# A decoder layer's self-attention: P.V in two passes over stacked high and low values, the output product behind the projection unit, and the latents turned one batch later

## What is computed

```
q = (x @ Wq.T).reshape(b, t, H, DH).transpose(0, 2, 1, 3)      # 32 heads of 16
k = (x @ Wk.T).reshape(b, t, HKV, DH).transpose(0, 2, 1, 3)    # 8 key/value heads of 16
v = (x @ Wv.T).reshape(b, t, HKV, DH).transpose(0, 2, 1, 3)
q = q * cos + _rotate_half(q) * sin
k = k * cos + _rotate_half(k) * sin
scores = jnp.einsum('bhgtd,bhkd->bhgtk', qg, k) / math.sqrt(DH)
attn = jax.nn.softmax(jnp.where(causal, scores, min), axis=-1)
ctx = jnp.einsum('bhgtk,bhkd->bhgtd', attn, v)
return ctx.transpose(...).reshape(b, t, E) @ Wo.T
```

## Time and profile before

| | |
|---|---|
| median of 3 runs | 1007.19 us (1006.62 to 1007.50) |
| the profiled execution | 1007.50 us, of which its span 1005.8 us |
| PE busy | 995.6 us (99% of the span) |
| DVE, ACT, POOL busy | 641.4, 559.5, 519.8 us (64%, 56%, 52%) |
| self-attention's batches | from 37.7 us to about 287 us, 29.83 us each in the middle |
| granted TensorE clock | 0.999 of full speed |

### The profile page before, as it was taken

One profiled execution on the slowest core, in us unless ns is written; L12 is line 12 of the kernel. 1 busy time (PEld: TensorE's weight loads), 2 busy tenths in 40 slices (PEclk: granted clock), 3 DMA queues, 4 the chain that ended last, 5 costly groups with the idle time before them and its releaser, 6 DMA issues.

```text
span 1005.8 us, 16102 instructions
## 1 busy us (share of the span) xinstructions
PE 995.6 (99%) x5552; PEld 836.7 (83%) x5552; DVE 641.4 (64%) x1224; ACT 559.5 (56%) x1695; POOL 519.8 (52%) x529
## 2 busy tenths in 40 slices
PE   8999999999999999999999999999999999999997
PEld 7777777777788888888888888888888888899996
DVE  6888888888433786555655655555555566655654
ACT  5766667666534665555656556555655667422221
POOL 3645444444231786665755756576666568512220
PEclk9999999999999999999999999999999999999999
DMA  9410111104454313233213313322332245100000
GB/s 343 119 29 15 43 42 44 42 22 124 135 157 119 95 57 102 74 95 105 86 61 105 105 64 106 92 76 94 95 105 75 83 139 168 62 22 21 21 22 21
DMA packets 74857, 85.15 MB, mean 85 GB/s; under 512 B 4512, under 2 KB 54688, under 8 KB 74784
## 3 DMA queue, kind: packets, MB, share of 16 engines
q1 hardware_dynamic: 74784, 84.21, 26.2%
HBM read 65.32 MB, written 18.87 MB: 84 GB/s over the span
## 4 chain that ended last, share of the span: by engine, by line
PE 92%; DVE 3%; ACT 2%; DMA 1%; issue 1%; POOL 1%; SPq 1%; DVEq 0%; POOLq 0%; ACTq 0%
PE bank L237 23%; PE bank L239 22%; PE bank L238 22%; PE bank L1143 11%; PE bank L1187 5%; PE bank L903 3%; PE bank L864 1%; PE bank L868 1%; DMA rawO<-in_L_attn_Wo_dram 1%; PE bank L871 1%; PE bank L874 1%; ACT Pb L1424 0%; DVE Kbdl L1696 0%; PE bank L817 0%; PE bank L810 0%
## 5 line engine op out<-in xcount | busy, mean ns | idle before, releaser
L673 POOL TENSOR_TENSOR Pb<-Pb,b_rec 128x512 f32<-128x512 f32 x128 | 135.5, 1059 | 200.6 <-DVE b_rec L1848 200.5
L1424 ACT ACTIVATE Pb<-bank,b_nb 128x256 f32<-128x256 f32 x256 | 119.1, 477 | 14.3 <-DVE b_nb L1843 14.2
L1843 DVE TENSOR_REDUCE b_nb<-bank 128x2 f32<-128x512 f32 x128 | 88.1, 688 | 59.2 <-PE bank L239 58.4
L635 POOL TENSOR_TENSOR Pa<-Pa,a_rec 128x512 f32<-128x512 f32 x64 | 68.2, 1066 | 102.1 <-DVE a_rec L1727 101.5
L1342 ACT ACTIVATE Pa<-bank,a_nb 128x128 f32<-128x128 f32 x256 | 90.8, 370 | 45.5 <-DVE a_nb L1721 44.8
L1285 ACT ACTIVATE PTh<-bank 128x512 fp32r<-128x512 f32 x128 | 76.3, 596 | 67.1 <-PE bank L1187 67.1
L237 PE MATMUL bank<-WOh,Oh 128*128 128x512 f32 x256 | 111.3, 435 | 0.0
L1597 DVE TENSOR_TENSOR PTl<-bank,PTh 128x512 fp32r<-128x512 f32 x128 | 87.7, 686 | 22.3 <-ACT PTh L1285 22.2
L239 PE MATMUL bank<-WOh,Ol 128*128 128x512 f32 x256 | 101.0, 395 | 0.0
L238 PE MATMUL bank<-WOl,Oh 128*128 128x512 f32 x256 | 100.4, 392 | 0.0
L1285 ACT ACTIVATE Oh<-bank 128x512 fp32r<-128x512 f32 x64 | 38.3, 599 | 91.4 <-PE bank L239 91.4
(11 more groups left out here) (279 smaller groups left out, 3008.6 us busy)
## 6 DMA issues: line engine op xcount, KB each, us to landing
KV<-kv_scratch SPq DMA_DIRECT2D x64, 512.0 KB, 3.4
kv_scratch<-KVst SPq DMA_DIRECT2D x64, 256.0 KB, 3.1
raw<-in_L_xattn_Wo_dram SPq DMA_DIRECT2D x32, 256.0 KB, 3.9
raw<-in_L_xattn_Wq_dram SPq DMA_DIRECT2D x24, 256.0 KB, 3.2
cx<-in_ctx_dram SPq DMA_DIRECT2D x8, 256.0 KB, 8.9
raw_first<-in_L_xattn_Wq_dram SPq DMA_DIRECT2D x8, 256.0 KB, 4.6
raw<-in_L_ffn_up_w_dram SPq DMA_DIRECT2D x8, 256.0 KB, 3.9
raw<-in_L_ffn_down_w_dram SPq DMA_DIRECT2D x8, 256.0 KB, 3.5
```

Source lines behind the costliest of these rows:

```text
L635: gp.tensor_tensor(pj, pj, a_rec[:, SG * j:SG * j + SG].unsqueeze(2).to_broadcast([P, SG, P]), ALU.mult).then_inc(g_norm, 1)
L673: gp.tensor_tensor(pk, pk, b_rec[:, k % 4, :].unsqueeze(2).to_broadcast([P, 2, KEYS]), ALU.mult).then_inc(b_g_norm, 1)
L1424: op = act.activation(Pb[:, k % 4, h, :], bank[k % 3][:, h * KEYS:(h + 1) * KEYS], ACT.Exp, bias=b_nb[:, k % 4, h:h + 1], scale=1.0, accum ...
L1843: dve.tensor_reduce(b_nb[:, k % 4, :], bank[k % 3][:].rearrange("p (h k) -> p h k", h=2), AX.X, ALU.max, negate=True).then_inc(b_v_nb, 1)
```

## The change

- **Values.** `Vst` replaces `Vbdh` and `Vbdl`: one 128 by 128 block for each head, the head's high parts at its own 16 columns and its low parts 64 columns away. For j from 0 to 3 the high parts fill rows 0 to 63 of bank 7 and the low parts rows 64 to 127; for j from 4 to 7 bank 4 takes it, the other way round. So a step has two products, with PTah and with PTal, in place of three.
- **Fold.** ACT copies the rows with the low parts (OLa, OLb), and `add_low(n)`, a product of 64 rows with a swapped identity (L960 of the changed file), adds them to the other half of the bank: `add_low(0)` at step 6, `add_low(1)` behind `scores(b + 1, 0)`. ACT and DVE then split each half of 64 partitions (OTh, OTl have tiles of their own now).
- **Order at the end of a batch.** The tail unit stands ahead of the output product and waits for OTl's first half; the output product waits for the second.
- **Latents.** `turn_latents(b)` moves from the end of batch b to step 2 of batch b + 1 (in the last batch to step 0, where ACT evicts it ahead of probabilities 3); ACT's and DVE's parts move along. `turn_xn` goes ahead of the unit of step 0, and its eviction and low part go forward: DVE's `xnTl` stands ahead of reciprocal 2.
- **Keys.** `turn_k` uses bank 3. The fourth block of Kbdl is made by POOL behind `normalise(b, 2)`.
- **Behind the last batch** `first_queries(1)` and `(2)` each stand one place further forward, and SP's load of `gate_w` waits for the output product instead of P.V.

```diff
-        VBW = P + SD
-        Vbdh = sb("Vbdh", "F", 0, [SKV * VBW], F32R)
-        Vbdl = sb("Vbdl", "F", 4.5, [SKV * VBW], F32R)
-        OTh, OTl = PTah[:, 0, :], PTal[:, 0, :]
+        Vst = sb("Vst", "F", 0, [SKV, P], F32R)
+        OTh = sb("OTh", "F", 4, [D], F32R)
+        OTl = sb("OTl", "F", 6, [D], F32R)
+        swap_r = sb("swap_r", "ST", 6, [P], F32R)
+        LOWER, UPPER = slice(0, 64), slice(64, P)
+        OLa, OLb = OTl[UPPER, :], PTah[LOWER, 0, :]
...
                 for j in range(2, SKV):
                     normalise(b, j)
+                    if j == 2:
+                        gp.wait_ge(v_qkl, 2 * b + 2)
+                        src = f32(KTl[:, KC - 1, :]).unsqueeze(1).to_broadcast([P, SG, P])
+                        gp.tensor_tensor(Kbdl[:, KC - 1, :].rearrange("p (c k) -> p c k", c=SG), src,
+                                         bd_mask[:].unsqueeze(2).to_broadcast([P, SG, P]), ALU.mult).then_inc(g_kbl, 1)
...
             def turn_k(b):
                 pe.wait_ge(v_qr, 2 * b + 2)
+                if b:
+                    pe.wait_ge(a_exp, SKV * b)
                 for m in range(KC):
-                    op = pe.transpose(bank[4][:, m * P:(m + 1) * P], kr[:, m * P:(m + 1) * P], ident[:])
+                    op = pe.transpose(bank[3][:, m * P:(m + 1) * P], kr[:, m * P:(m + 1) * P], ident[:])
...
-                pe.wait_ge(v_kbd, KC * b + m + 1)
+                if m < KC - 1:
+                    pe.wait_ge(v_kbd, (KC - 1) * b + m + 1)
+                else:
+                    pe.wait_ge(g_kbl, b + 1)
...
                 def values(j):
+                    bk = bank[7] if j < 4 else bank[4]
                     if j == SKV - 1:
                         for n, split in enumerate((v_ptl_half, v_ptl)):
                             pe.wait_ge(split, SKV * b + SKV if n else b + 1)
                             cols = slice(n * KEYS, (n + 1) * KEYS)
-                            op = split3(pe, bank[7][:, cols], Vbdh[:, j * P:(j + 1) * P], Vbdl[:, j * P:(j + 1) * P],
-                                        PTah[:, j % 2, cols], PTal[:, j % 2, cols], False, n == 1)
+                            pe.matmul(bk[:, cols], Vst[:, j, :], PTah[:, j % 2, cols], start=False, stop=False)
+                            op = pe.matmul(bk[:, cols], Vst[:, j, :], PTal[:, j % 2, cols], start=False, stop=n == 1)
                         op.then_inc(pe_pv, 1)
                         return
                     pe.wait_ge(v_ptl, SKV * b + j + 1)
@@ -919,8 +945,20 @@
                         pe.wait_ge(v_vl, b + 1)
                         pe.wait_ge(v_ul, U_B0 + 2 * b)
-                    op = split3(pe, bank[7][:], Vbdh[:, j * P:(j + 1) * P], Vbdl[:, j * P:(j + 1) * P],
-                                PTah[:, j % 2, :], PTal[:, j % 2, :], j == 0, False)
+                    if j == 4:
+                        pe.wait_ge(a_exp, SKV * b + 6)
+                    pe.matmul(bk[:], Vst[:, j, :], PTah[:, j % 2, :], start=j % 4 == 0, stop=False)
+                    op = pe.matmul(bk[:], Vst[:, j, :], PTal[:, j % 2, :], start=False, stop=j == 3)
+                    if j == 3:
+                        op.then_inc(pe_pv, 1)
+                def add_low(n):
+                    pe.wait_ge(a_ol, 2 * b + n + 1)
+                    bk, rows, low = ((bank[7], UPPER, OLa), (bank[4], LOWER, OLb))[n]
+                    pe.matmul(bk[:], swap_r[rows, :], low, start=False, stop=True,
+                              skip_group_check=True).then_inc(pe_sw, 1)
...
                         pe.wait_ge(v_qkl, 2 * b + 1)
+                        pe.wait_ge(v_vl, b + 1)
+                        if not last:
+                            if b == 0:
+                                pe.wait_ge(v_ctl, 6)
+                            else:
+                                turn_xn(b + 1)
                         unit(U_B0 + 2 * b)
-                        if not last:
-                            if b:
-                                pe.wait_ge(v_htl, b)
-                            else:
-                                pe.wait_ge(v_ctl, 6)
-                            turn_xn(b + 1)
+                        if b == 0:
+                            turn_xn(1)
+                        if last:
+                            turn_latents(b - 1)
                         scores(b, 2)
...
                         q_product((0, 1))
+                        if b:
+                            turn_latents(b - 1)
                     if j == 3:
                         scores(b, 3)
                         if not last:
                             q_product((2, 3))
                     if j == 4 and not last:
+                        if b:
+                            pe.wait_ge(v_htl, b)
                         kv_product(range(KC))
                     if j == 6 and not last:
                         turn_q(b + 1)
+                    if j == 6:
+                        add_low(0)
...
+                add_low(1)
+                tail = U_E0 - 1 if last else U_B0 + 2 * b + 1
+                pe.wait_ge(v_ol, 2 * b + 1)
+                if b:
+                    pe.wait_ge(v_htl, b)
+                unit(tail)
+                pe.wait_ge(v_ol, 2 * b + 2)
                 for g in range(SG):
-                    if g % 2 == 0:
-                        pe.wait_ge(v_ol if g else v_ol_half, b + 1)
                     op = split3(pe, bank[6][:], OTh[:, g * P:(g + 1) * P], OTl[:, g * P:(g + 1) * P], SOh[:, g, :],
                                 SOl[:, g, :], g == 0, g == SG - 1)
                 op.then_inc(pe_wo, 1)
                 if not last:
                     scores(b + 1, 1)
-                unit(U_E0 - 1 if last else U_B0 + 2 * b + 1)
-                if not last:
-                    pe.wait_ge(v_vl, b + 2)
-                else:
+                if last:
                     first_queries(0)
+                    first_queries(1)
                     pe.wait_ge(v_ul, U_L0 + 7)
-                turn_latents(b)
...
-            first_queries(1)
+            first_queries(2)
             pe.wait_ge(v_htl, NB)
             unit(U_E0)
             unit(U_E0 + 1)
@@ -1100,7 +1154,6 @@
             unit(U_E0 + 2)
             unit(U_E0 + 3)
             unit(U_E0 + 4)
-            first_queries(2)
             first_queries(3)
...
                     hi(PTah[:, j % 2, :], bank[5 + j % 2][:]).then_inc(a_pt, 1)
+                    if j == 0 and last:
+                        latents_hi(b - 1)
+                    if j == 0 and b and not last:
+                        xn_hi(b + 1)
+                    if j == 5:
+                        act.wait_ge(pe_pv, 2 * b + 1)
+                        hi(OLa, bank[7][UPPER, :]).then_inc(a_ol, 1)
+                    if j == 7:
+                        if not last:
+                            k_hi(b + 1)
+                        act.wait_ge(pe_sw, 2 * b + 1)
+                        hi(OTh[LOWER, :], bank[7][LOWER, :]).then_inc(a_o, 1)
                     if j + 3 < SKV:
                         probs(b, j + 3)
                     if j == 0:
                         unit_hi(U_B0 + 2 * b)
-                        if not last:
-                            xn_hi(b + 1)
+                    if j == 0 and b == 0:
+                        xn_hi(1)
+                    if j == 2 and b and not last:
+                        latents_hi(b - 1)
                     if j in LAST_STEPS and last:
                         unit_hi(LAST_STEPS[j])
                     if j == 6 and not last:
                         q_hi(b + 1)
-                if not last:
-                    k_hi(b + 1)
-                act.wait_ge(pe_pv, b + 1)
-                hi(OTh, bank[7][:]).then_inc(a_o, 1)
+                act.wait_ge(pe_pv, 2 * b + 2)
+                hi(OLb, bank[4][LOWER, :]).then_inc(a_ol, 1)
                 if not last:
                     values_hi(b + 1)
+                act.wait_ge(pe_sw, 2 * b + 2)
+                hi(OTh[UPPER, :], bank[4][UPPER, :]).then_inc(a_o, 1)
+                if not last:
                     for j in range(3):
                         probs(b + 1, j)
                 else:
@@ -1376,7 +1444,8 @@
                         first_wq(h)
                     unit_hi(U_L0 + 6)
                 unit_hi(U_E0 - 1 if last else U_B0 + 2 * b + 1)
-                latents_hi(b)
+                if last:
+                    latents_hi(b)
...
+                cells = Vst[:].rearrange("p a (b d) -> p (a b) d", d=SD)
+                for n in range(2):
+                    js = slice(4 * n, 4 * n + 4)
+                    first = 4 * n * (SKV + 1)
+                    at_lo = first + (-4 if n else 4)
+                    op = lo(cells[:, at_lo:at_lo + 3 * (SKV + 1) + 1:SKV + 1, :],
+                            bank[0][:, P:2 * P].rearrange("p (j d) -> p j d", j=SKV)[:, js, :],
+                            cells[:, first:first + 3 * (SKV + 1) + 1:SKV + 1, :])
+                op.then_inc(v_vl, 1)
...
```

(21 more changed lines are left out.)

33 lines of the change are left out of this document (18 added, 15 removed).

## The result

The changed kernel takes 1020.64 us (median of 4 runs, 1019.93 to 1021.59) against 1007.21 us before: a ratio of 1.013, 95% interval 1.0118 to 1.0142, so it is 13.4 us slower. The profiled execution took 1021.59 us, its span 1019.9 us, against 1007.50 and 1005.8 us.

What follows compares the result with a forecast made beforehand. PE bound the kernel before; the change would make a ring over DVE's queue the bound. 11.0 + 1.0 - 0.6 - 0.4 - 0.8 = +10.2 us gave 1017.4 us against the median, range 1014 to 1021.

Steps and rivals of the forecast that it cites:

- ring over DVE: Turn(7), residual, reciprocal 6, turn(6), next turn(7): 9.96 + 18.9 + 1.4 + 1.78 = 32.0 us, setting the batch's length.
- from reciprocal 6 to turn(6): Third part of the round, followed over POOL's 1.08 us of work and a semaphore's hop: 1.4 us.
- turn(6) to turn(7): Last part of the round on PE: 1.68 us, less 0.23, plus 0.33 for add_low(0), giving 1.78 us.
- What PE saves: PE per batch: 1.84 us of dropped products, less new products and lost savings, leaves 1.1 us if nobody keeps it waiting.
- PE's waits: PE in each batch waits 3.3 us, at turn(2), turn(5), values(4) for PTal, and turn(6).
- The five rings: From batch 0's turn(7) to batch 5's, five rounds together add 11.0 us.
- The last batch: Its units give each step slack, so it saves some 0.8 us: 1.84 less new products and one wait for XTl.
- Behind the last turn(7): Work after the last batch is only reordered, with the same product count behind the residual: 0 us.
- A: Rival: PE stays the bound and each batch gives 1.1 us, so 998.4 us; chance 0.14.
- B: Rival: DVE's waits for ACT at XTl might vanish (-1.4 us), leaving some 0.7 us a batch, 1011 us; chance 0.09.
- C: Rival: waits drop TensorE's clock to 1.2 GHz, up to 28 us more per affected batch; chance 0.02.
- D: Rival: waits fall elsewhere, such as a late OTl half before the tail unit, 0.5 us a batch, 1021 us; chance 0.07.

Runs made afterwards that it cites:

- d1: Changed kernel plus two unused maxima on DVE (0.6 us each) behind the residual's statistics in every batch but the last: 1028.65 us.
- d2: Changed kernel plus two unused maxima on DVE (0.6 us each) ahead of its wait for the output product: 1020.42 us.
- p1: Changed kernel plus a third pass on PE in the values of steps 0 to 4, every batch but the last: 1022.94 us.
- x5: Changed kernel with half the tail unit either side of the output product, reciprocal 2 ahead of maxima 3, XTl behind maxima 7, a later batch's statistics early: 1010.71 us.
- u2: Kernel before, three passes kept, with only the new order: tail unit ahead of the output product, latents in step 2 of the next batch: 1023.27 us.
- y1: Changed kernel keeping two-pass values and smaller edits, with unit, latents and turn_xn put back where they were before: 1018.46 us.
- x3: Changed kernel with a later batch's statistics (1.1 us) moved into DVE's wait for the output product: 1017.32 us.
- x4: Changed kernel with XTl moved behind maxima 6 and 7 and a later batch's statistics moved into DVE's wait for the output product: 1015.22 us.
- x2: Changed kernel with DVE's low part of the latents (XTl) moved from behind reciprocal 4 to behind maxima 6 and 7: 1014.54 us.
- x1: Changed kernel with the output product back ahead of the tail unit, the unit behind scores(1), two-pass values kept: 1024.29 us.
- u1: Kernel before, three passes kept, with only the tail unit moved ahead of the output product in every batch but the last: 1038.37 us.

## Why the prediction was right, and where it was off

- **The bound moves from PE to a ring over DVE.** Right: PE is idle for 2.5 us in a batch, DVE's waits of 1.89 and 1.39 us as forecast (about 2 and 1.44), and added work counts on DVE behind the residual (d1: 1.17 of 1.2 us) and not ahead of it (d2) or on PE (p1, but for one pass).
- **The ring's length.** 32.24 measured, 32.0 predicted. Three parts are within 0.1 us, one of them partly by luck: from reciprocal 6 to turn(6) the prediction followed POOL, while p1 shows that the path over PTal(4) and values(4) counts, which happens to be as long. The fourth, turn(6) to turn(7), was 1.99 in place of 1.78: add_low(0) costs 185.72 - 185.29 = 0.43 us, where the prediction counted one change of rows for both ends and took 0.33, and the turn of the queries ahead of it went from 0.45 to 0.53. The two new products cost 0.43 + 0.32 = 0.75 us, where my sum had 0.56. By the rule of the Trainium skill that a change of mode drains the array (TensorEngine Tiling (Array Packing), Key Properties) the prediction's estimate was 0.6 us more than its 0.56. The measured 0.75 us lie nearer to the row's 0.1 us for each change.
- **What PE saves.** This term was wrong, and only the ring hid it. Predicted 1.1 us a batch; measured 29.83 - 29.69 = 0.14 in the changed kernel, and 0.28 in x5. From start to start over one batch, waits taken off: the values fell from 6.20 to 4.96 us (4.52 in x5, so 1.24 to 1.68 of the 1.84 counted), the swap products added 0.75 (0.56 counted), and the eight turns of the probabilities rose from 3.04 to 3.61 us, which was not counted at all. The order alone lengthens PE's own work: u2, with the same products as before, has 30.47 us of it against 29.83. By form, the two passes save 30.47 - 29.69 = 0.78 us in the new order and 29.83 - 29.33 = 0.50 us in the old one (y1, 30.98 less waits of 1.65). A turn between two products takes 0.36 us, next to another transpose, behind 64-row products or around a wait 0.41 to 0.65, and there are now more of these.
- **PE's waits.** Predicted at turn(2), turn(5), values(4) and turn(6), 3.3 us in all; measured at the first three 0.95 + 0.47 + 0.86, none at turn(6), and 0.24 behind turn(7), where before the step was longer by 0.18 (0.41 less 0.23).
- **The sum.** Predicted +10.2 us, measured +14.1 between the two profiled executions and +13.4 between the medians; 1020.64 us lie only 0.4 us inside the range of 1014 to 1021. The five rings gave 218.52 - 57.38 - 149.17 = +12.0 (+11.0 predicted) and batch 6 +1.3 (+1.0). Batch 0 from its turn(0) to its turn(7) took 18.05 us in place of 19.40, -1.35 (-0.6 predicted). Ahead of it stand +1.6 us (39.33 against 37.71) that can't be told from the spread of the start: in kernels with the same code up to there this turn(0) comes anywhere from 37.08 (x3) to 40.83 us (x4). From batch 6's turn(7) to the next turn(0) it was -0.36, as forecast (-0.4). The largest miss lies behind that. The last batch from turn(0) to turn(7) is +0.27 (27.07 against 26.81) where -0.8 was predicted: the values fell by 1.36 us, but the swap product took 0.42, the turn of batch 6's latents, which stood ahead of turn(0) before, 0.35, the turns of the probabilities 0.48 more, and the wait for XTl 0.21; the rest lies in the units and the scores. Behind the last turn(7) it is +0.65 (731.92 against 731.27) in place of 0, and +0.36 to +0.90 in the six other kernels with the same code there (d1, d2, p1, x2, x3, x4). What makes this part longer is not shown: it adds up bit by bit, with no new wait of PE.
- **Rivals.** A (PE stays the bound) fell with d1 and p1. B (XTl's wait vanishes by itself) did not happen; x2 shows that it was worth 1.2 us a batch. C, the clock: full throughout the self-attention of the changed kernel, whose waits are 0.95 us at most. But it was no far-fetched danger: x1, y1 and u1 are three neighbours of this kernel where it did fall, at a price of 1.5 to 1.6 us for each fall in x1 and y1, not the 28 us of my rival. D named a wait that did not come, though the time it gave, 1021, is the measured one.

No version beat the kernel before. The best, x5, is 0.15 to 0.34% slower. The order can be repaired, but PE then has almost as much to do as before, so that little is left to win.

## What to carry to other kernels

Before moving work on the bounding engine, ask whom it covers: the unit behind the output product hid the normalisation of the latents, and the same unit ahead of it delayed everything that stood on DVE behind the residual. Follow the ring once round through each in-order queue and add its terms; it forecast the batch to 0.2 us, whereas the forecast of PE's saving from the count of passes was wrong by a factor of four to eight. A cheap test of such a ring is a dummy instruction on either side of a wait: where it costs its full length you are inside, where it costs nothing you are outside.
